# Two attention layers on one core: sums of two head groups at once, token maxima subtracted on VectorE, and another order of units in four slots

## The chip, the cores and the metric

The kernel runs on one core of one Trainium2 chip. The metric is the device time of one execution in microseconds (us). A core has TensorE (PE in the profile, its weight loads PEld), VectorE (DVE), ScalarE (ACT), GpSimd (POOL) and SyncE (SP), which run side by side, each through its own instructions in program order, and wait for each other on semaphores.

## The reference

Sixteen independent batches, each 112 query rows by 320 features, and a context of 375 rows by 192. Two layers of cross attention follow each other. Layer 0 has 8 heads of 40; of the 375 context rows the last 4 are tokens. Cut to what matters:

```python
# layer 0
hs      = mha(x @ Wq, enc @ Wk, enc @ Wv)            # enc: 371 rows, 8 heads
ca_q1   = einsum('btc,th->bch', ca, Wq_ca)[:, indices]
ca_hs1  = mha(ca_q1, x, x)                           # 112 x 112 scores, 8 heads
ca_hs2  = mha(ca_hs1 @ Wq, ca @ Wk_ca, ca @ Wv_ca)   # 4 tokens
x1      = (hs + ca_hs2) @ Wout + b_out + x
# layer 1: 20 heads of 16 over all 375 context rows
out     = mha(x1 @ Wq, ctx @ Wk, ctx @ Wv) @ Wo + bo + x1
```

## The kernel before, in words

The program is one software pipeline over the batches. An iteration `t` has seven slots. Each slot scores one **group** of four heads: slots 0 and 1 take the two groups of layer 0 of batch t (here a0, a1), slots 2 to 6 the five groups of layer 1 of batch t-1 (b0 to b4). A group passes through the engines in stages, one slot apart:

- `scores` (L1156, L1159): TensorE computes queries by keys, two heads (a pair) at a time, into the two PSUM banks `bankS`. VectorE takes the row maxima (`maximum`, L773) after each pair. The second pair may start only when the maxima of the first are taken.
- one slot later `transpose_m` (L1172) turns the negated maxima into a row, VectorE copies it out (`copy_mT`, L779) and a DMA places it as one more row of the queries.
- two slots later (`LAG` is 2) `shifted_scores` (L1187, L1193) computes keys by queries with the maximum already subtracted, ScalarE takes the exponentials (`exps`, L573, L574, L577), `attend` (L1225) multiplies them with the values into `bankO`, and VectorE copies the result out (`copy_o`, L790).

Between these stages stand the **units**: projections, transposes and small products (K1_0 is part 0 of the keys of layer 1, V0_1 part 1 of the values of layer 0, q0 the queries, q1T_0 a transpose of part of them, N0, N1a and N1b the transposes of the attention sums before they are divided by the sums of exponentials, out0 and out1 the output projections). All units share two PSUM banks, `bankX`, in turn: a unit gets the bank that the unit two before it in the written order had, and waits until ScalarE or VectorE, or one after the other, has emptied it. The order is written out by hand in the table `UNITS`: for each slot four phases of units, with the offset of the batch. On TensorE a slot runs

```python
scores(g, 0); units of phase 0; shifted_scores(late); transpose_m(before)
units of phase 1; scores(g, 1); units of phase 2; attend(late); units of phase 3
```

VectorE's slot is: maxima of pair 0, what phase 0 needs, `copy_mT`, phase 1, maxima of pair 1, phase 2, `copy_o`, phase 3. ScalarE's is: phase 0, `exps`, the DMA of the maxima, phases 1 to 3.

The drains that matter below: q1T is rounded by ScalarE (L666), then multiplied by VectorE (L829). q0 and q1 are rounded by ScalarE (L648, L653), the remainder is taken by VectorE (L765). K0 and K1 go through ScalarE (L625, L619) and VectorE (L814, L809), and DMAs then stack them for the scores of the next iteration (`stack_k0` on SP, L347; `stack_k1` on SP and GpSimd).

The 112 x 112 softmax of layer 0 are the units S2_0 and S2_1 (L1111), four heads each. VectorE takes the maxima (L837); then ScalarE runs one exponential per head with the maximum as bias and a sum beside it (L595), and this empties the bank. `reciprocal2` (L877) turns the sums over, GpSimd scales (`normalise2`, L464), and T2_0, T2_1 transpose. S3 and p3T are the four tokens' part; `normalise3` is its softmax's division (three small instructions, L881 to L885).

Of the kernel before, what the change touches and what calls it, by code (L numbers as in the profile page):

```python
# [7 lines left out]
ALU = mybir.AluOpType  # L8
# [51 lines left out]
    ([], [("T2_0", 0), ("T2_1", 0)], [("V0_0", 0), ("V0_1", 0), ("q0", 1)], [("V0_2", 0), ("PV2", 0), ("K1_0", 0)]),  # L60
# [25 lines left out]
NUMBER = {g: n for n, g in enumerate(GROUPS)}  # L86

# [24 lines left out]
def xattn_kernel(nc, xT, xpad, ctxT, caS, caT, w_all, w_ca, wqT, bd96, consts, bias, out):  # L112
    g_rows = nc.dram_tensor("g_rows", [B, 3, 32, HID], F32, kind="Internal").ap()

    with ExitStack() as ctx:
# [101 lines left out]
        bank_mT = bankO[0:GROUP, 0:SQ]  # L217
# [57 lines left out]
        rsum2_done = sem("rsum2_done")  # L275
        prob2_ready = sem("prob2_ready")
# [275 lines left out]
        def _(act):  # L552
# [10 lines left out]
            def exps(g):  # L563
# [4 lines left out]
                if n >= 2:  # L568
                    act.wait_ge(pv_done, n - 1)
                elif n == 1:  # L570
                    act.wait_ge(w_split, parts_split[2])
# [19 lines left out]
            def exps2(b, half):  # L591
                act.wait_ge(max2_done, 2 * b + half + 1)
                X = bankX[bank(f"S2_{half}", b)]
                for h in range(4 * half, 4 * half + 4):
                    last = nc.scalar.activation(prob2[0:SQ, h, :], X[0:SQ, (h % 4) * SQ:(h % 4 + 1) * SQ], ACT.Exp,  # L595
                                                bias=negmax2[:, h:h + 1], accum_out=sum2[:, h:h + 1])
                last.then_inc(bank_drained[bank(f"S2_{half}", b)], 1)

            def unit(name, b):
# [27 lines left out]
                elif kind == "V0":  # L627
                    if i == 0 and b == 0:
                        act.wait_ge(zeroed, 3)
                    elif i == 0:  # L630
                        act.wait_ge(pv_done, NUMBER[0, b - 1, 1] + 1)
# [3 lines left out]
                elif kind == "V1":  # L635
                    if i == 0 and b < 2:
                        act.wait_ge(zeroed, 6 + b)
                    elif i == 0:
                        act.wait_ge(pv_done, NUMBER[1, b - 2, G1 - 1] + 1)
# [91 lines left out]
        def _(dve):  # L731
# [49 lines left out]
            def copy_o(g):  # L781
                layer, b, k = g
                n = NUMBER[g]
                dve.wait_ge(pv_done, n + 1)
                if layer == 0:
                    dst, src = o0T[:, 2 * k:2 * k + 2, :].rearrange("p c q -> p (c q)"), bankO[:, 0:2 * SQ]
                else:
                    at = (2 + n % 2) * SQ
                    dst, src = o1T[:, k, :], bankO[:, at:at + SQ]
# [554 lines left out]
```

## Time and profile before

| what | value |
|---|---|
| median of three runs | 756.53 us (755.18 to 759.52) |
| the profiled execution | 753.38 us, span 751.5 us |
| TensorE busy | 703.0 us, 94% of the span |
| VectorE busy | 472.3 us, 63% |
| ScalarE busy | 404.0 us, 54% |
| GpSimd busy | 295.5 us, 39% |
| mean granted TensorE clock | 0.983 of full speed |

The span is what lies between the first and last instruction of the profile; the execution's own time is 1.9 us longer. TensorE's share is that of matmuls in flight, whose records overlap, so it is no measure of how fast it works, but what it leaves is time in which nothing was in flight.

### The profile page before, as it was taken

The page shows a single profiled execution, that of the slowest core. Times are in us where ns is not written, and L with a number is a line of the kernel's source. Part 1 is how long each engine was busy: PE and PEld are TensorE (multiplying, and loading weights), DVE is VectorE, ACT ScalarE, POOL GpSimd, SP SyncE. Part 2 cuts the span into 40 slices and gives each one's busy share as a digit, 9 for nine tenths or more (in the row PEclk, how much of TensorE's full clock was granted, in tenths as well). Part 3 has the DMA queues.
Part 4 walks back from the last instruction along what each step waited for, and adds up shares of the span by engine and source line. Part 5 has one row for each costly group of instructions (what it writes and reads, how often), then busy time and mean ns, then how long its engine had stood idle before and what let it go on. Part 6 is the DMA issues. An engine that isn't in the chain of part 4 may idle for free.

```text
span 751.5 us, 18194 instructions
## 1 busy us (share of the span) xinstructions
PE 703.0 (94%) x6924; PEld 610.3 (81%) x6924; DVE 472.3 (63%) x1028; ACT 404.0 (54%) x923; POOL 295.5 (39%) x401
## 2 busy tenths in 40 slices
PE   8787999999999999999999999999999999999975
PEld 5586888888888888888888888888888888888763
DVE  2653666657576665757576575756667575766662
ACT  2454555555565555565555555556555555654432
POOL 5485662444334253433325344323524542330300
PEclk9889999999999999999999999999999999999996
DMA  9533553443516244252524434261533425051400
GB/s 325 175 96 96 112 133 75 107 80 79 133 47 143 62 119 95 67 118 54 137 60 125 92 80 103 62 142 45 136 81 94 89 76 129 20 137 28 87 7 11
DMA packets 52387, 72.45 MB, mean 96 GB/s; under 512 B 12128, under 2 KB 44256, under 8 KB 52304
## 3 DMA queue, kind: packets, MB, share of 16 engines
q1 hardware_dynamic: 44832, 60.34, 31.7%
q0 software_dynamic: 6144, 9.25, 6.5%
q10 hardware_dynamic: 1328, 1.71, 0.6%
q8 instruction: 57, 0.93, 0.5%
q14 instruction: 26, 0.21, 0.1%
HBM read 20.60 MB, written 4.26 MB: 33 GB/s over the span
## 4 chain that ended last, share of the span: by engine, by line
PE 69%; ACT 13%; DVE 8%; issue 3%; POOL 1%; DMA 1%; SPq 1%; ACTq 0%; POOLq 0%
PE bankX L1005 28%; PE bankO L1225 8%; PE bankST L1193 7%; ACT arena L577 7%; PE bankS L1159 6%; PE bankST L1187 5%; ACT arena L595 3%; DVE negmax L773 2%; DVE q1T L829 2%; PE bankX L1118 2%; PE bankX L1125 2%; PE bankX L1087 2%; PE bankS L1156 2%; ACT q1T L666 2%; PE bankX L1071 2%
## 5 line engine op out<-in xcount | busy, mean ns | idle before, releaser
L773 DVE TENSOR_REDUCE negmax<-bankS 112x2 f32<-112x750 f32 (+1 forms) x224 | 208.7, 932 | 57.0 <-PE bankS L1159 32.7
L494 POOL DMA_DIRECT2D k_stack<-stage x192 | 96.6, 511 | 181.5 <-DVE stage L809 153.9
L577 ACT ACTIVATE arena<-bankST 125x1344 f32<-125x1344 f32 x80 | 103.5, 1294 | 30.9 <-PE bankST L1193 30.9
L1225 PE MATMUL bankO<-arena,v 125*32 125x112 f32 (+2 forms) x2688 | 107.2, 264 | 6.2 <-ACT arena L577 4.4
L1225 PEld LDWEIGHTS bankO<-arena,v 125*32 125x32 f32 (+2 forms) x2688 | 81.2, 117 | 29.0 <-issue 12.7
L1159 PE MATMUL bankS<-k_stack,q1T 112*112 112x376 f32 x320 | 87.8, 355 | 4.1 <-DVE negmax L773 3.0
L1005 PE MATMUL bankX<-ctx_hi,WH 128*120 128x376 f32 (+2 forms) x192 | 69.0, 360 | 3.0 <-DVE qn L765 2.2
L457 POOL TENSOR_TENSOR w2bd<-w2s,cst 96x896 fp32r<-96x896 f32 x16 | 29.9, 1870 | 98.4 <-DVE w2s L765 98.4
L1005 PE MATMUL bankX<-WH,ctx_hi 128*125 128x320 f32 x192 | 66.1, 344 | 0.1
L1193 PE MATMUL bankST<-q1T,k_stack 112*125 112x224 f32 x480 | 65.4, 272 | 0.0
L1005 PE MATMUL bankX<-ctx_hi,WL 128*120 128x376 f32 (+2 forms) x192 | 64.0, 334 | 0.0
L1193 PEld LDWEIGHTS bankST<-q1T,k_stack 112*125 112x125 f32 x480 | 62.0, 188 | 0.8 <-DMA q1T<-mT 0.4
L1005 PE MATMUL bankX<-WL,ctx_hi 128*125 128x320 f32 x192 | 58.5, 312 | 0.0
L1159 PEld LDWEIGHTS bankS<-k_stack,q1T 112*112 112x112 f32 x320 | 49.4, 177 | 8.8 <-DVE negmax L773 6.5
L829 DVE TENSOR_SCALAR q1T<-bankX,odd_rows 128x448 fp32r<-128x448 f32 (+1 forms) x48 | 29.1, 606 | 41.7 <-ACT q1T L666 41.2
L595 ACT ACTIVATE arena<-bankX,negmax 112x112 f32<-112x112 f32 x128 | 43.6, 354 | 21.7 <-DVE negmax L837 21.6
L1005 PE MATMUL bankX<-WH,act_hi 128*112 128x320 f32 x144 | 46.7, 325 | 3.3 <-DVE act_hi L866 1.4
L483 POOL TENSOR_TENSOR xb<-xp,bias_sb 112x320 f32<-112x320 f32 x16 | 13.9, 867 | 88.7 <-DVE x L860 88.6
L779 DVE CAST mT<-bankO 4x112 fp32r<-4x112 f32 x112 | 29.0, 259 | 30.0 <-PE bankO L1172 30.0
L1187 PEld LDWEIGHTS bankST<-q0T,k_stack 121*125 121x125 f32 (+1 forms) x384 | 46.0, 187 | 0.0
L619 ACT ACTIVATE stage<-bankX 128x376 fp32r<-128x376 f32 (+1 forms) x48 | 23.1, 482 | 41.7 <-PE bankX L1005 41.0
L1187 PE MATMUL bankST<-q0T,k_stack 121*125 121x112 f32 (+1 forms) x384 | 44.9, 266 | 0.0
(141 smaller groups left out, 1545.8 us busy)
## 6 DMA issues: line engine op xcount, KB each, us to landing
k_stack<-stage SPq DMA_DIRECT2D x96, 176.2 KB
k_stack<-stage SPq DMA_DIRECT2D x192, 70.5 KB, 2.6
k_stack<-stage POOLq DMA_DIRECT2D x192, 47.0 KB, 2.0
ctx_raw<-in_ctxT SPq DMA_DIRECT2D x16, 376.0 KB, 3.3
k_stack<-stage SPq DMA_DIRECT2D x48, 117.5 KB
xp<-in_xpad SPq DMA_DIRECT2D x16, 224.0 KB, 3.3
x_raw<-in_xT SPq DMA_DIRECT2D x16, 168.0 KB, 2.4
out<-x1b SPq DMA_DIRECT2D x16, 140.0 KB, 3.2
```

The costliest lines, as they stand in the source:

```text
L457: nc.gpsimd.tensor_tensor(w2bd[:, :, :], w2s[:, :].bitcast(F32).unsqueeze(1).broadcast_to((96, H0, SQ)), mask96.unsqueeze(2).broadcast_to( ...
L494: pool.dma_start(dst, src).then_inc(k1_stacked_pool[b % 2], 16)
L577: nc.scalar.activation(dst[0:KC], bankST[0:KC, :, 0:GROUP * SQ], ACT.Exp).then_inc(exp_done, 1)
L595: last = nc.scalar.activation(prob2[0:SQ, h, :], X[0:SQ, (h % 4) * SQ:(h % 4 + 1) * SQ], ACT.Exp, bias=negmax2[:, h:h + 1], accum_out=sum2 ...
L773: nc.vector.tensor_reduce(negmax[:, n % 2, 2 * pair:2 * pair + 2], bankS[0:SQ, :, 0:keys], axis=AX, op=ALU.max, negate=True).then_inc(max_ ...
L779: nc.vector.tensor_copy(mT[:, n % MT_BUFS, :], bank_mT).then_inc(mT_copied, 1)
L829: nc.vector.tensor_scalar(q1T[:, 4 * i:4 * i + g, 1, :], X[:, 0:g * SQ].rearrange("p (h q) -> p h q", h=g), odd_rows[:, :], None, ALU.mult ...
L1005: last = nc.tensor.matmul(dst, lhs, rhs, start=(n == 0), stop=(n == len(passes) - 1))
L1159: last = nc.tensor.matmul(bankS[0:SQ, j, 0:SKP], q1T[0:ROWS1, h // 2, h % 2, :], k1_stack[b % 2][0:ROWS1, h // 2, :], start=True, stop=True)
L1187: last = nc.tensor.matmul(bankST[0:keys, c, SQ * j:SQ * j + SQ], k0_stack[0:M_ROW0 + 1, h, KC * c:KC * c + keys], q0T[0:M_ROW0 + 1, h, :], ...
L1193: last = nc.tensor.matmul(bankST[0:KC, c, 2 * SQ * pair:2 * SQ * pair + 2 * SQ], k1_stack[b % 2][0:ROWS1, 2 * k + pair, KC * c:KC * c + KC ...
L1225: last = nc.tensor.matmul(dst, v, src[0:keys, c, SQ * j:SQ * j + SQ], start=(c == 0), stop=(c == NKC - 1))
```

## The change

It has five parts.

1. `attend` and `copy_o` work on an **episode**: the two groups of layer 0 together, of layer 1 groups 0 and 1, 2 and 3, and 4 alone. An episode is attended in the slot in which its last group's turn comes: slot 3 (a0, a1), slot 5 (b0, b1), slot 0 (b2, b3), slot 1 (b4). Semaphores count episodes.
2. The transposed maxima move from `bankO` to spare columns of the second bank of `bankS`. `transpose_m` therefore waits for the maxima of pair 0 of the group that is being scored now, and the second matmul of each `scores` waits for `copy_mT`. `attend` and `transpose_m` no longer wait for each other's copies.
3. In S2 VectorE subtracts the maxima while it copies the scores out of the bank (an added tensor_tensor of 112 x 448 for each half), which frees the bank; ScalarE then runs one exponential of 448 columns in place for each half.
4. `reciprocal2` sums the exponentials on VectorE first (an added reduction of 112 x 896) and stands at the end of slot 3; it stood in slot 4, behind `copy_mT`.
5. The table of units is another one in slots 1 to 4, and the first slots likewise.

```diff
 UNITS = [
     ([("V1_0", -1)], [("q1T_0", -1)], [("V1_1", -1)], [("W2", 1), ("PV2", 0)]),
-    ([("q1T_1", -1), ("V1_2", -1)], [("q1T_2", -1)], [("q0", 1)], [("N1a", -2), ("K1_0", 0)]),
-    ([("K1_1", 0)], [("S3", 0), ("S2_0", 1)], [("N1b", -2)], [("S2_1", 1)]),
-    ([("K1_2", 0)], [("K0_0", 1)], [("hn1T", -2)], [("K0_1", 1)]),
-    ([("K0_2", 1)], [("p3T", 0), ("N0", 0)], [("out1", -2)], [("q0T_0", 1)]),
+    ([("q1T_1", -1), ("V1_2", -1)], [("q1T_2", -1), ("N1a", -2)], [("q0", 1)], [("S2_0", 1)]),
+    ([("K1_0", 0)], [("S3", 0)], [("N1b", -2), ("S2_1", 1)], [("K1_1", 0)]),
+    ([("K1_2", 0)], [("K0_0", 1)], [("hn1T", -2)], []),
+    ([("K0_1", 1)], [("out1", -2)], [("p3T", 0), ("N0", 0)], [("K0_2", 1), ("q0T_0", 1)]),
     ([("hn0T", 0), ("V0_0", 1)], [("q0T_1", 1)], [("out0", 0)], [("T2_0", 1)]),
     ([("x1T", 0), ("V0_1", 1)], [("T2_1", 1)], [("q1", 0)], [("V0_2", 1)]),
 ]
 FIRST_SLOTS = [
     ([], [], [], [("W2", 1)]),
-    ([], [("T2_0", 0), ("T2_1", 0)], [("V0_0", 0), ("V0_1", 0), ("q0", 1)], [("V0_2", 0), ("PV2", 0), ("K1_0", 0)]),
+    ([], [("T2_0", 0), ("T2_1", 0)], [("V0_0", 0), ("V0_1", 0), ("q0", 1)], [("V0_2", 0), ("PV2", 0)]),
+    ([("K1_0", 0)], [("S3", 0)], [("S2_0", 1)], [("K1_1", 0), ("S2_1", 1)]),
 ]
...
+EPISODES = [e for b in range(B + 1) for e in
+            ([[(0, b, 0), (0, b, 1)]] if b < B else []) +
+            ([[(1, b - 1, 0), (1, b - 1, 1)], [(1, b - 1, 2), (1, b - 1, 3)], [(1, b - 1, 4)]] if b > 0 else [])]
+EPISODE = {g: n for n, e in enumerate(EPISODES) for g in e}
...
-        bank_mT = bankO[0:GROUP, 0:SQ]
+        bank_mT = bankS[0:GROUP, 1, SKP + 8:SKP + 8 + SQ]
...
             def exps2(b, half):
-                act.wait_ge(max2_done, 2 * b + half + 1)
-                X = bankX[bank(f"S2_{half}", b)]
-                for h in range(4 * half, 4 * half + 4):
-                    last = nc.scalar.activation(prob2[0:SQ, h, :], X[0:SQ, (h % 4) * SQ:(h % 4 + 1) * SQ], ACT.Exp,
-                                                bias=negmax2[:, h:h + 1], accum_out=sum2[:, h:h + 1])
-                last.then_inc(bank_drained[bank(f"S2_{half}", b)], 1)
+                act.wait_ge(bank_drained[bank(f"S2_{half}", b)], drained(f"S2_{half}", b))
+                scores2 = prob2[0:SQ, 4 * half:4 * half + 4, :].rearrange("p h k -> p (h k)")
+                nc.scalar.activation(scores2, scores2, ACT.Exp).then_inc(exp2_done, 1)
...
+                    nc.vector.tensor_tensor(
+                        prob2[0:SQ, 4 * i:4 * i + 4, :], X[0:SQ, 0:4 * SQ].rearrange("p (h k) -> p h k", h=4),
+                        negmax2[:, 4 * i:4 * i + 4].unsqueeze(2).broadcast_to((SQ, 4, SQ)), ALU.add).then_inc(free, 1)
...
             def reciprocal2(b):
-                dve.wait_ge(bank_drained[bank("S2_0", b)], drained("S2_0", b))
-                dve.wait_ge(bank_drained[bank("S2_1", b)], drained("S2_1", b))
+                dve.wait_ge(exp2_done, 2 * b + 2)
+                nc.vector.reduce_sum(sum2[:, :], prob2[0:SQ], axis=AX).then_inc(sum2_done, 1)
+                dve.wait_ge(sum2_done, b + 1)
                 nc.vector.reciprocal(rsum2[:, :], sum2[:, :]).then_inc(rsum2_done, 1)
...
-                    if i == 4 and t + 1 < B:
-                        reciprocal2(t + 1)
...
-                    if late:
-                        copy_o(late)
+                    if attended_at(t, i):
+                        copy_o(attended_at(t, i))
                     for u in units_of(t, i, 3):
                         unit(*u)
                     if i == 2 and t < B:
                         normalise3(t)
                     if i == 3 and t < B:
                         split_p3(t)
+                    if i == 3 and t + 1 < B:
+                        reciprocal2(t + 1)
...
                 for j in range(2):
                     h = GROUP * k + 2 * pair + j
+                    if j == 1 and transposed > 0:
+                        pe.wait_ge(mT_copied, transposed)
...
-            def transpose_m(g, attended):
+            def transpose_m(g, scoring):
                 n = NUMBER[g]
-                pe.wait_ge(max_done, 2 * n + 2)
+                if scoring:
+                    pe.wait_ge(max_done, 2 * NUMBER[scoring] + 1)
+                else:
+                    pe.wait_ge(max_done, 2 * n + 2)
                 if n > 0:
                     pe.wait_ge(mT_copied, n)
-                else:
-                    pe.wait_ge(g_split, 4)
-                if attended > 0:
-                    pe.wait_ge(o_copied, attended)
```

The matmuls of `attend` are the same and as many, in the same order within a group.

## Rows read from the trace of the kernel before

**Rows 1.** The page's head: span, and busy time, share and instructions by engine.
```profile
span 751.5 us, 18194 instructions
PE 703.0 (94%) x6924; PEld 610.3 (81%) x6924; DVE 472.3 (63%) x1028; ACT 404.0 (54%) x923; POOL 295.5 (39%) x401
```

**Rows 2.** Timeline of PE over iteration 7: start, duration, instruction, idle before it.
```profile
329.13 0.51 PE L1156 MATMUL bankS<-k_stack,q0T 120*112 120x372 f32 x2
...
333.54 0.82 PE L1105 MATMUL bankX<-x_raw,bd 128*96 128x112 f32 x6 [0.25 <-DVE q1T L829]
...
338.13 0.31 PE L1005 MATMUL bankX<-WH,x_hi 128*112 128x320 f32 x1
...
340.93 0.45 PE L1005 MATMUL bankX<-ctx_hi,WH 128*128 128x376 f32 x1 [0.17 <-DVE qn L765]
...
347.86 0.46 PE L1111 MATMUL bankX<-w2bd,ca_st 96*112 96x448 f32 x1 [0.33 <-ACT arena L595]
...
357.27 0.65 PE L1095 MATMUL bankX<-cst,o0T 128*112 128x128 f32 x4 [0.49 <-DVE stage L814]
...
370.93 0.78 PE L1225 MATMUL bankO<-arena,v 125*32 125x112 f32 x24
...
372.48 0.50 PE L1156 MATMUL bankS<-k_stack,q0T 120*112 120x372 f32 x2
```

**Rows 3.** The chain that ended last, in order of time, same iteration.
```profile
346.35 1.46 ACT arena L595 x8
...
348.31 0.35 PE bankS L1159 x2
348.66 0.85 PE bankX L1005 x5
349.51 1.24 PE bankST L1187 x12
...
352.35 1.31 PE bankO L1225 x24
...
362.67 0.65 PE bankST L1193 x6
```

**Rows 4.** Timeline of ACT, slot 1 of the iteration.
```profile
337.62 1.29 ACT L577 ACTIVATE arena<-bankST 125x1344 f32<-125x1344 f32 x1 [0.21 <-PE bankST L1193]
...
338.81 0.34 ACT L666 ACTIVATE q1T<-bankX 64x224 fp32r<-64x224 f32 x1
```

**Rows 5.** Timeline of DVE, same iteration.
```profile
339.18 0.45 DVE L829 TENSOR_SCALAR q1T<-bankX,odd_rows 128x224 fp32r<-128x224 f32 x1 [1.21 <-ACT q1T L666]
...
347.29 0.22 DVE L797 TENSOR_TENSOR hn<-bankX,r 112x64 f32<-112x64 f32 x1
...
371.77 0.49 DVE L765 SCALAR_TENSOR_TENSOR qn<-bankX,qn 112x320 fp32r<-112x320 f32 x1 [0.97 <-ACT qn L653]
```

**Rows 6.** Groups of instructions: busy us, mean ns of one, then idle before.
```profile
L773 DVE TENSOR_REDUCE negmax<-bankS 112x2 f32<-112x750 f32 (+1 forms) x224 | 208.7, 932 | 57.0 <-PE bankS L1159 32.7 <-PE bankS L1156 24.2
...
L790 DVE COPY o1T<-bankO 128x112 f32<-128x112 f32 x80 | 21.5, 269 | 12.9 <-PE bankO L1225 12.9
...
L837 DVE TENSOR_REDUCE negmax<-bankX 112x4 f32<-112x448 f32 x32 | 19.8, 620 | 5.8 <-PE bankX L1111 5.7
...
L574 ACT ACTIVATE arena<-bankST 121x448 f32<-121x448 f32 x32 | 17.2, 538 | 0.0
...
L790 DVE COPY o0T<-bankO 128x224 f32<-128x224 f32 x32 | 12.5, 392 | 3.2 <-PE bankO L1225 2.0
...
L860 DVE TENSOR_TENSOR x<-bankX,xb 112x320 f32<-112x320 f32 x16 | 7.9, 492 | 7.9 <-PE bankX L1005 7.9
...
L885 DVE TENSOR_TENSOR p<-p,rsum 112x32 f32<-112x32 f32 x16 | 3.1, 191 | 0.6
```

**Rows 7.** Timeline of SP, same iteration.
```profile
357.29 8.46 SPq L347 DMA_DIRECT2D k_stack<-stage  x9
```

**Rows 8.** DMA issues by line: count, KB each, median us to landing.
```profile
k_stack<-stage SPq DMA_DIRECT2D x192, 70.5 KB, 2.6
```

More of the change, by code:

```diff
@@ L275, in xattn_kernel @@
         rsum2_done = sem("rsum2_done")
+        exp2_done = sem("exp2_done")
+        sum2_done = sem("sum2_done")
         prob2_ready = sem("prob2_ready")
@@ L911, in _ @@
                 for i in range(SLOTS):
-                    g, before, late = scored_at(t, i), scored_at(t, i, 1), scored_at(t, i, LAG)
+                    g, before = scored_at(t, i), scored_at(t, i, 1)
                     if g:
@@ L1090, in unit @@
                     layer, k = {"N0": (0, 1), "N1a": (1, 3), "N1b": (1, 4)}[kind]
-                    pe.wait_ge(o_copied, NUMBER[layer, b, k] + 1)
+                    pe.wait_ge(o_copied, EPISODE[layer, b, k] + 1)
                     cols = [o0T[:, c, :] for c in range(4)] if layer == 0 else [
@@ L1135, in unit, with scores @@
                 last.then_inc(unit_filled, 1)
-            def scores(g, pair):
+            def scores(g, pair, transposed):
                 layer, b, k = g
@@ L1225, in attend @@
-                    last = nc.tensor.matmul(dst, v, src[0:keys, c, SQ * j:SQ * j + SQ], start=(c == 0),
-                                            stop=(c == NKC - 1))
+                        at_once = [(c, j) for pair in range(2) for c in range(NKC) for j in (2 * pair, 2 * pair + 1)]
+                    else:
+                        at_once = [(c, j) for c in range(NKC) for j in range(GROUP)]
+                    for c, j in at_once:
+                        h = GROUP * k + j
+                        if layer == 0:
+                            keys = KC if c < 2 else KC - NTOK
+                            at = (2 * k + j // 2) * SQ
+                            dst = bankO[64 * (j % 2):64 * (j % 2) + 64, at:at + SQ]
+                            v = v0[0:keys, c, 64 * h:64 * h + 64]
+                        else:
+                            keys = KC
+                            at = (2 + k % 2) * SQ
+                            dst = bankO[32 * j:32 * j + 32, at:at + SQ]
+                            v = v1[b % 2][0:keys, c, 32 * h:32 * h + 32]
+                        last = nc.tensor.matmul(dst, v, src[0:keys, c, SQ * j:SQ * j + SQ], start=(c == 0),
+                                                stop=(c == NKC - 1))
@@ L1249, in _ @@
                     if g:
-                        scores(g, 0)
+                        scores(g, 0, transposed)
                     for u in units_of(t, i, 0):
@@ L1255, in _ @@
                     if before:
-                        transpose_m(before, attended)
+                        transpose_m(before, g)
                         transposed = NUMBER[before] + 1
@@ L1260, in _ @@
                     if g:
-                        scores(g, 1)
+                        scores(g, 1, transposed)
                     for u in units_of(t, i, 2):
                         unit(*u)
-                    if late:
-                        attend(late, transposed)
-                        attended = NUMBER[late] + 1
+                    if attended_at(t, i):
+                        attend(attended_at(t, i))
                     for u in units_of(t, i, 3):
```

58 lines of the change are left out of this document (26 added, 32 removed).

## The prediction

> **What bounds the kernel now.** I read the page's head first, then TensorE's timeline over one whole iteration, then what filled each gap there on the other engines. The head says that something is in flight on TensorE for 94% of the span, VectorE is busy for 63% and ScalarE for 54% [rows 1]. So TensorE's order of work sets the time, and another engine matters only where TensorE stands and waits for it. One iteration takes 372.48 - 329.13 = 43.35 us [rows 2], and the iterations 1 to 14, the full ones, repeat it.
>
> The timeline shows four places in it where TensorE is empty [rows 2]: W2 waits 0.25 us for VectorE's drain of q1T_0; K1_0 waits 0.17 for VectorE's drain of q0; S2_1 waits 0.33 for ScalarE's eight instructions of S2_0, which take 1.46 us in all [rows 3]; N0 waits 0.49 for VectorE's drain of K0_2. All four are the same thing: a unit waits for its turn of `bankX`, because the unit two before it has not been emptied. They add up to 1.24 us. Matmuls overlap by some 0.15 us at each of these places, and some waits are too short to empty the engine, so I estimate what such waits cost at 2.4 us of the 43.35, with 1.24 as the lower bound.
>
> **The change part by part.** TensorE's matmuls stay as they are. What can change is only the waiting, so I walk through an iteration in the new order, with a unit's two-before neighbour looked up each time.
>
> *What is removed.* In the new order W2 has 24 more matmuls of an episode ahead of it (the second group adds about 0.7 us, from the duration 0.78 in [rows 2]), and its 0.25 goes. S2_0's bank is free after two VectorE instructions, the 0.620 maxima [rows 6] and the subtraction. I take 0.62 for that too: 320 columns take 0.492 and the step from 112 to 224 columns of a copy costs 0.123, 1.1 ns a column [rows 6], so 448 give 0.63. That replaces 1.46 on ScalarE, and S2_1 no longer stands directly behind. N0 now has out1 two before it instead of K0_2. All of the 2.4 us goes. Three of seven changeovers into `attend` go as well: no row prices one, it lies between nothing and a matmul's own latency of about 0.26, and I take 0.1 each and 0.35 in all with those behind it. Removed: 2.75 us, bounds 1.2 and 3.2.
>
> On ScalarE eight instructions per half become one of 0.54 [rows 6], worth about 1 us each half. It was idle beside TensorE there, so this is worth nothing by itself. On VectorE copies shrink (a copy of 448 columns is about 0.64 instead of two of 0.392 [rows 6]), some 0.4 us less an iteration; the two subtractions add 1.25, the reduction over 896 columns about 1.09 (0.932 for 750 [rows 6] and 146 more at 1.1 ns; 1.11 if all of it scales). VectorE is idle for some 16 us of an iteration (37%, [rows 1]), so the question is only where these stand.
>
> *New wait 1, q0 behind q1T_2.* The order was q1T_1, V1_2, q1T_2, q0, so q0 had V1_2 two before it. It becomes q1T_1, V1_2, q1T_2, N1a, q0: q0 has q1T_2 before it. That one's drain is late, because ScalarE reaches it only behind `exps` of b4: those start at 337.62, q1T_2's at 338.81 [rows 4], VectorE's part starts 339.18 and ends 339.63 [rows 5]. Nothing ahead of this moves. q0 started at 338.13 [rows 2]; with N1a's four transposes (0.65, of which 0.26 overlaps what follows) in front it could start at 338.5, and must now wait until 339.7. Cost 1.15 us. This is the surest of all terms: both times are read.
>
> *New wait 2, K1_1 behind N1b.* In slot 2 the order is K1_0, S3, N1b, S2_1, K1_1, and no `attend` stands in that slot any more. N1b is emptied by VectorE only behind the maxima of b0's second pair: 0.932, then a reciprocal of about 0.2 and a product of 0.22 [rows 5, 6], with handoffs 1.45 us after the scores end. TensorE has N1b and S2_1 to do meanwhile, under 0.5 us. Cost 0.95, bounds 0.6 and 1.1.
>
> *New wait 3, transposing the maxima in slot 3.* `transpose_m` now waits for the maxima of the group just scored. In slot 3 these are queued on VectorE behind: maxima and subtraction of S2_1 (1.25), the wait for ScalarE, which is in order itself and does the exponential of S2_1 (0.54) before it rounds K1_1 (0.5 for 376 columns against 0.54 for 448), VectorE's part of K1_1 (0.55: 0.492 and 56 columns more), `normalise3` (three at 0.19), and their own 0.932 [rows 6]. Together 4.2 us from the end of N1b's drain, with some overlap. TensorE, released by that same drain, has K1_1, scores, K1_2 and the shifted scores: 0.9 + 0.35 + 0.85 + 1.24 [rows 3], 3.4 us with a changeover. Cost 0.8, bounds 0.4 and 1.1. Behind the waiting transpose stands everything on TensorE.
>
> *New wait 4, the same in slot 4.* The double `attend` of layer 0 (twice 1.31 [rows 3]) ends slot 3. Behind it VectorE must copy 448 columns (0.64), split p3 (0.19), sum 896 columns (1.09), take the reciprocal (0.2), and only then take the maxima of b2's first pair (0.932): 3.0 us. TensorE has scores, K0_1 and the shifted scores of b0: 0.35 + 0.9 + 0.65 [rows 3], 2.0 us. Cost 1.05, bounds 0.6 and 1.2. The Trainium skill ("VectorE: DVE Perf Modes", Rules for kernel authors) advises to expect 1x of `tensor_reduce` on a hot path and calls it the slowest VectorE operation; its cycle table (The AWS errata-adjusted cycle table, same page) would give 0.99 us as an estimate for this one, so by the page this wait would be 0.95. No row here has the reduction itself.
>
> *Smaller ones.* V1_0 waits for q1, whose drain the `attend` of slot 6 [rows 2] used to cover: VectorE ends it at 371.77 + 0.49 [rows 5], TensorE would be there 0.36 earlier. N0 now follows out1 and scores so closely that its bank is 0.3 late. K0_2 moves from before N0 to the end of slot 4, and hn0T, two behind it, has only q0T_0 and scores as cover: 0.4. q0T_0 behind N0 0.15; slot 2's S2_1 behind S3 and K1_0 0.25. Together 1.45, bounds 0.7 and 2.0. The second matmul of each `scores` waits for `copy_mT`, which comes 0.6 us after the transpose, just when a unit of transposes and one matmul have passed; I take nothing, and 0.1 in each of three slots as the bound.
>
> *Sum.* Added 1.15 + 0.95 + 0.8 + 1.05 + 1.45 = 5.4, removed 2.75: 2.65 us an iteration. Fourteen full iterations: 37 us. At the two ends I estimate 2 more: in the last slots, with no units, `copy_mT` (about 0.26, the size of the 0.269 copy [rows 6]) now stands between the maxima of the two pairs, for five groups, and the first reciprocal waits for a reduction. The profiled execution took 753.38 us, so 792.5; the median of the runs shown is 3 us above it. I predict 795.
>
> **The rivals.**
>
> *Faster: the new waits are covered.* The place is VectorE's queue in slots 2 to 4: if it ran ahead of TensorE there, waits 2 to 4 would vanish, and if ScalarE took q1T_2 ahead of `exps`, wait 1 too. Then only the removals count: 2.75 x 14 = 38, 718 us. The point from which it decides is added waits under 2.75 an iteration. For it speaks that VectorE is idle 37% of the time [rows 1]; against it that each queue is strictly in order and wait 1 alone, read from recorded times, takes 1.15 of it. Somewhere between (waits at their lower bounds, removals at their upper) lies 756 to 762. The Trainium skill ("Perfetto Trace Analysis", Identifying the Most-Contended Engine) ranks engines by occupancy and has the busiest optimised first; by that alone, work moved to an engine at 63% would cost nothing and this rival would hold.
>
> *Slower by less: waits 3 and 4 fall away.* If the second one's reduction and the drains of S2 run shorter than the rows suggest, or if TensorE arrives later for another reason, 1.85 an iteration goes: 795 - 26 = 769.
>
> *Slower by more: stacking K0 comes late.* K0_2's drain moves some 6 us later. The nine DMAs of `stack_k0` take 8.46 us to issue on SP [rows 7], behind that drain, and the last lands 2.6 us after its issue [rows 8]. By the walk they land less than 1 us before the next a0 is scored. If it takes 2 us more, each iteration is 1 us longer: 809.
>
> *It does nothing:* the two sides cancel, 753 to 760.
>
> **How the numbers follow.** Forecast with its own range 778 to 806: 0.66. K0 late: 0.10. Waits 3 and 4 gone: 0.10. Nothing: 0.05. Faster: 0.09. A change under 0.5%, 3.8 us, can't be told from none by a measurement of this kernel. The range takes in the first three cases: 764 to 812. Faster 0.09, same 0.05, slower 0.86.
>
> **What the profile after would show.** An iteration of about 46 us. TensorE empty before q0 for some 1.1 us with VectorE's L829 as the one waited for; before K1_1, for the drain of N1b; before the transpose of the maxima in slots 3 and 4, for the maxima, 0.8 and 1.0; none of the four gaps of now. VectorE busy some 30 us longer, ScalarE some 50 shorter. The prediction is wrong if the transposes find the maxima done, or if the iteration is 43 or less.

## The result, and the profile after

| | before | changed |
|---|---|---|
| median of five runs | 755.85 us (754.58 to 759.52) | 807.72 us (806.28 to 813.15) |
| profiled execution, span | 753.38, 751.5 us | 813.15, 811.3 us |
| mean granted TensorE clock | 0.983 | 0.952 |

The ratio is 1.0688, interval 1.0644 to 1.0732: slower by 52 us, where the forecast was 39. The median lies outside the forecast's own range of 778 to 806 and inside the outer one, which reached to 812. The profiled execution of the changed kernel was its slowest run, 5.4 us above the median.

The head of the page of the changed kernel, to set beside [rows 1]:

```profile
span 811.3 us, 17904 instructions
PE 726.3 (90%) x6924; PEld 629.5 (78%) x6924; DVE 502.6 (62%) x1028; ACT 375.5 (46%) x699; POOL 294.6 (36%) x401
```

VectorE is busy 30 us longer, ScalarE 28.5 shorter. The forecast said 50, but its own working (about 1 us less for each of 32 halves) gives 32. TensorE has as many matmuls and is in flight 23 us longer; the reason for that comes below.

TensorE's timeline over one iteration, to set beside [rows 2]:

```profile
312.79 0.82 PE L1124 MATMUL bankX<-x_raw,bd 128*96 128x112 f32 x6
...
317.39 0.59 PE L1177 MATMUL bankS<-k_stack,q0T 120*112 120x372 f32 x2
318.93 0.40 PE L1024 MATMUL bankX<-WH,x_hi 128*112 128x320 f32 x1 [0.95 <-DVE q1T L841]
...
325.44 0.46 PE L1130 MATMUL bankX<-w2bd,ca_st 96*112 96x448 f32 x1
326.73 0.44 PE L1024 MATMUL bankX<-ctx_hi,WH 128*128 128x376 f32 x1 [0.83 <-DVE hn L809]
...
330.88 0.26 PE L1192 MATMUL bankS<-cst,negmax 112*4 112x112 f32 x1 [0.59 <-DVE negmax L786]
...
332.63 2.54 PE L1248 MATMUL bankO<-arena,v 125*64 125x112 f32 x48
...
338.03 0.26 PE L1192 MATMUL bankS<-cst,negmax 112*4 112x112 f32 x1 [0.82 <-DVE negmax L786]
...
340.11 0.65 PE L1114 MATMUL bankX<-cst,o0T 128*112 128x128 f32 x4
...
342.75 0.51 PE L1106 MATMUL bankX<-cst,hn 112*128 112x112 f32 x3 [0.22 <-DVE stage L826]
...
354.11 0.57 PE L1177 MATMUL bankS<-k_stack,q0T 120*112 120x372 f32 x2 [0.31 <-issue]
```

The four gaps of before are gone: W2 (312.79) follows its attend without one, K1_0, S2_1 (325.44) and N0 (340.11) too. In their place stand four others, each at the named place: q0 waits 0.95 us for VectorE's part of q1T_2; K1_1 waits 0.83 for N1b's drain; the transposes of the maxima in slots 3 and 4 wait 0.59 and 0.82. Counted from where the instruction could have started they cost a little more, as a matmul's latency overlaps the rest: q0 could have gone at 317.80 (the scores start at 317.39 and take 0.41), and goes 1.13 later.

VectorE's timeline shows what is queued in front of the last two:

```profile
326.45 0.22 DVE L809 TENSOR_TENSOR hn<-bankX,r 112x64 f32<-112x64 f32 x1
...
327.24 0.62 DVE L855 TENSOR_TENSOR arena<-bankX,negmax 112x448 f32<-112x448 f32 x1
328.87 0.55 DVE L821 TENSOR_TENSOR stage<-bankX,stage 128x376 fp32r<-128x376 f32 x1 [1.01 <-ACT stage L632]
...
329.90 0.93 DVE L786 TENSOR_REDUCE negmax<-bankS 112x2 f32<-112x750 f32 x1
...
335.21 0.62 DVE L802 COPY o0T<-bankO 128x448 f32<-128x448 f32 x1 [0.55 <-PE bankO L1248]
335.75 0.18 DVE L910 TENSOR_TENSOR p3w<-p,p3w 112x32 fp32r<-112x32 f32 x1
335.85 1.08 DVE L894 TENSOR_REDUCE sum<-arena 112x8 f32<-112x896 f32 x1
336.97 0.20 DVE L896 RECIPROCAL rsum<-sum 112x8 f32<-112x8 f32 x1
337.09 0.89 DVE L786 TENSOR_REDUCE negmax<-bankS 112x2 f32<-112x750 f32 x1
```

Before 329.90 it sits idle for 1.01 us itself, for ScalarE's rounding of K1_1, and the maxima stand behind that. Before 337.09 stand the copy, the split, the sum and the reciprocal. The three operations that no row of before had came out as estimated: 0.62 (0.62), 0.62 (0.64) and 1.08 (1.09). For the sum the cycle table of the Trainium skill ("VectorE: DVE Perf Modes", The AWS errata-adjusted cycle table) gives an estimate of 0.99 us; the trace has 1.08, so here the table is 0.09 short.

I take an iteration from the first matmul of W2 in it to that in the next. Between iterations 1 and 14 there are thirteen such stretches. The first, in which the pipeline isn't yet full, takes 43.1 us (before 40.6). Of the twelve full iterations behind it four take 46.1 us and eight 46.6 to 47.2; before it was 43.3 in all twelve. The difference between the two kinds is in the clock. The windows by stretch (length, busy time of the five engines, granted clock, DMA), first two whole iterations, then two short stretches inside the second:

```profile
312.79:358.88 46.09, 42.23 (x431) 37.05 (x427) 30.30 (x64) 22.91 (x43) 17.11 (x24) 1.00 0.37 89
358.88:405.49 46.61, 43.35 (x432) 38.33 (x428) 30.41 (x64) 22.85 (x43) 17.09 (x24) 0.96 0.36 86
...
372.00:374.00 2.00, 1.18 (x4) 1.19 (x5) 1.88 (x5) 0.02 (x1) 0.00 (x0) 0.59 0.00 1
374.00:376.00 2.00, 2.00 (x9) 1.98 (x8) 0.66 (x3) 1.04 (x2) 0.00 (x0) 0.56 0.04 8
```

The clock fell while TensorE still waited for K1_1's bank (the wait ends at 372.82): in windows of half a microsecond it is 0.86 of full speed from 372.0, then 0.50, the lower of the two levels (1.2 GHz), until 375.5. Matmuls of 376 columns follow each other every 0.31 us instead of 0.17. Part of that time comes back: the transpose in slot 3, which then arrives late, no longer waits 0.59 for its maxima. This is also why TensorE's busy time grew with the same matmuls: a full iteration at the full clock is busy 42.2 us here and 42.0 before, the one from 358.88 on 43.35, and the rest of the growth is at the two ends, which come below.

### The profile page after: what moved, and what is told of

Read it like the earlier page. It is cut to its first block, busy times and chain, and to the rows that moved or that the text cites. A ratio compares the mean times of both kernels' runs of the same rounds, so it can differ in the third digit from the quotient of the medians.

```text
span 811.3 us, 17904 instructions
## 1 busy us (share of the span) xinstructions
PE 726.3 (90%) x6924; PEld 629.5 (78%) x6924; DVE 502.6 (62%) x1028; ACT 375.5 (46%) x699; POOL 294.6 (36%) x401
## 4 chain that ended last, share of the span: by engine, by line
PE 69%; DVE 15%; ACT 5%; issue 3%; POOL 1%; DMA 1%; SPq 1%; ACTq 0%; POOLq 0%
PE bankX L1024 27%; PE bankO L1248 11%; PE bankST L1213 5%; PE bankS L1180 5%; DVE negmax L786 5%; PE bankST L1207 4%; PE bankS L1177 3%; ACT arena L593 2%; PE bankX L1106 2%; DVE sum L894 2%; PE bankX L1137 2%; PE bankX L1144 2%; PE bankS L1192 2%; PE bankX L1152 1%; PE bankX L1097 1%
## 5 line engine op out<-in xcount | busy, mean ns | idle before, releaser
L1180 PE MATMUL bankS<-k_stack,q1T 112*112 112x376 f32 x320 | 96.4, 380 | 6.5 <-DVE negmax L786 4.1
L1248 PE MATMUL bankO<-arena,v 125*32 125x112 f32 (+2 forms) x2688 | 99.1, 265 | 2.7 <-ACT arena L593 2.7
L1024 PE MATMUL bankX<-ctx_hi,WH 128*120 128x376 f32 (+2 forms) x192 | 75.1, 391 | 12.8 <-DVE hn L809 10.8
L1024 PE MATMUL bankX<-ctx_hi,WL 128*120 128x376 f32 (+2 forms) x192 | 68.8, 358 | 0.0
L1180 PEld LDWEIGHTS bankS<-k_stack,q1T 112*112 112x112 f32 x320 | 53.4, 186 | 15.0 <-DVE negmax L786 6.6
L638 ACT ACTIVATE stage<-bankX 120x376 fp32r<-120x376 f32 (+1 forms) x48 | 23.2, 484 | 78.2 <-PE bankX L1024 78.2
L1024 PEld LDWEIGHTS bankX<-ctx_hi,WH 128*120 128x120 f32 (+2 forms) x192 | 37.8, 197 | 22.1 <-DVE hn L809 14.5
L1207 PEld LDWEIGHTS bankST<-q0T,k_stack 121*125 121x125 f32 (+1 forms) x384 | 48.8, 197 | 0.0
L1177 PE MATMUL bankS<-k_stack,q0T 120*112 120x372 f32 x128 | 39.0, 387 | 10.3 <-issue 8.4
L826 DVE TENSOR_TENSOR stage<-bankX,stage 120x376 fp32r<-120x376 f32 (+1 forms) x48 | 26.1, 544 | 34.4 <-ACT stage L638 34.4
```

Source lines behind the costliest of these rows:

```text
L826: nc.vector.tensor_tensor(k0_lo[0:rows, i, :].bitcast(F32R), X[0:rows, 0:SKP], k0_hi[0:rows, i, :], ALU.subtract).then_inc(free, 1)
L1024: last = nc.tensor.matmul(dst, lhs, rhs, start=(n == 0), stop=(n == len(passes) - 1))
L1177: last = nc.tensor.matmul(bankS[0:SQ, j, 0:SKE + 1], q0T[0:M_ROW0, h, :], k0_stack[0:M_ROW0, h, 0:SKE + 1], start=True, stop=True)
L1180: last = nc.tensor.matmul(bankS[0:SQ, j, 0:SKP], q1T[0:ROWS1, h // 2, h % 2, :], k1_stack[b % 2][0:ROWS1, h // 2, :], start=True, stop=True)
L1207: last = nc.tensor.matmul(bankST[0:keys, c, SQ * j:SQ * j + SQ], k0_stack[0:M_ROW0 + 1, h, KC * c:KC * c + keys], q0T[0:M_ROW0 + 1, h, :], ...
L1248: last = nc.tensor.matmul(dst, v, src[0:keys, c, SQ * j:SQ * j + SQ], start=(c == 0), stop=(c == NKC - 1))
```

## The experiments

Each kernel is compared with the kernel before on the same chip. The first W2 starts 17 to 18 us into the span in nine of the fourteen profiled executions and at 22 us in five, whatever the edit, and this moves a median by several microseconds. So beside the median I give the time of a full iteration, from W2 to W2, as the twelve of the profiled execution have it.

### One part at a time

**The new table of units alone.** The two tables as in the diff above, all else as before:

```diff
-    ([("q1T_1", -1), ("V1_2", -1)], [("q1T_2", -1)], [("q0", 1)], [("N1a", -2), ("K1_0", 0)]),
+    ([("q1T_1", -1), ("V1_2", -1)], [("q1T_2", -1), ("N1a", -2)], [("q0", 1)], [("S2_0", 1)]),
...
```

> The kernel before with the new table of units and first slots alone. Theory A (each wait comes from one part meeting another): of the new waits only q0 behind q1T_2 (1.1 us) and hn0T behind K0_2 (0.3) and late stacked K0 appear; K1_1's wait for N1b stays covered, since attend of a0 still stands in slot 2, and the transposes of the maxima wait for nothing. Against that go some 1.2 us of old waits. Net 0 to +1 us an iteration: 756 to 772, best 764. Rival B (the order alone carries the loss): 795 or more.

Measured: 781.64 us, ratio 1.0343 (1.0293 to 1.0394), an iteration 44.8. So the order alone costs 1.5 us an iteration; theory A named the right places, but 781.64 lies 10 us above its range: its 0 to 1 us an iteration was 0.5 to 1.5 too hopeful. Rival B (795 or more) falls. TensorE's timeline has q0 and hn0T where they were expected:

```profile
350.29 0.40 PE L1006 MATMUL bankX<-WH,x_hi 128*112 128x320 f32 x1 [0.95 <-DVE q1T L830]
...
365.64 0.60 PE L1160 MATMUL bankS<-k_stack,q1T 112*112 112x376 f32 x2 [0.36 <-DVE negmax L774]
...
373.13 0.51 PE L1088 MATMUL bankX<-cst,hn 112*128 112x112 f32 x3 [0.42 <-DVE stage L815]
```

q0's wait is 0.95 us here as in the changed kernel. It needs nothing but the new neighbour in the table.

**All but the table.** The changed kernel with the two tables of before:

```diff
-    ([("q1T_1", -1), ("V1_2", -1)], [("q1T_2", -1), ("N1a", -2)], [("q0", 1)], [("S2_0", 1)]),
+    ([("q1T_1", -1), ("V1_2", -1)], [("q1T_2", -1)], [("q0", 1)], [("N1a", -2), ("K1_0", 0)]),
...
```

> The changed kernel with the tables of before. Theory A: the wait of q0 and that of K1_1 for N1b go, the waits of the transposes for the maxima stay, the one in slot 4 longer (1.5 us, since VectorE's part of K0_1 now lies in front of the sum of 896 columns), and S2_1 has lost its cover in slot 2: 770 to 790. Rival B (order alone carries the loss): 750 to 758.

Measured: four runs of 846.8, 875.9, 877.2 and 879.1 us, with mean granted clocks of 0.90 in the first and 0.86 in the others. Both theories missed by far. What follows is read from the fastest of them. The waits came as theory A had them, the transpose of slot 4 and S2_1:

```profile
341.35 0.46 PE L1129 MATMUL bankX<-w2bd,ca_st 96*112 96x448 f32 x1 [0.87 <-DVE arena L854]
...
357.91 0.26 PE L1191 MATMUL bankS<-cst,negmax 112*4 112x112 f32 x1 [1.43 <-DVE negmax L785]
```

What nobody had priced is the clock. The windows of two whole iterations of the 846.8 us execution:

```profile
327.85:379.04 51.19, 48.19 (x431) 42.90 (x427) 30.36 (x64) 23.17 (x43) 17.16 (x24) 0.87 0.34 80
...
428.91:474.64 45.73, 42.38 (x431) 37.20 (x427) 30.24 (x64) 23.01 (x43) 17.16 (x24) 1.00 0.38 91
```

With the full clock the iteration takes 45.7, 2.4 more than before (two of the twelve); with the clock at half in parts of it, 48.2 to 51.2 (the other ten, mean clock 0.87 to 0.93). The waits cost 2.4, the slower clock up to 5.5. So the parts don't add up. The table costs 1.5 us an iteration on the kernel before, but only 0.4 on top of the other parts (46.1 against 45.7 at the full clock); and with it the granted clock in a full iteration of the change is 0.96 or 1.00. Without the table the change is slower still. Its two longest waits are 0.87 and 1.43 us, against 0.95 and 0.83 with it, but that this is why the clock differs is not shown.

**The subtraction on VectorE and the early sum alone.** Before, with parts 3 and 4 of the change:

```diff
-                    if i == 4 and t + 1 < B:
-                        reciprocal2(t + 1)
...
+                    if i == 3 and t + 1 < B:
+                        reciprocal2(t + 1)
```

> The kernel before with the subtraction on VectorE, one exponential for each half, and the sum of 896 columns at the end of slot 3, nothing else. Theory A: S2_1's 0.33 goes, N0 waits some 1 us longer for K0_2's drain, which VectorE reaches behind the sum: 0 to +1 us an iteration, 756 to 770, best 764. Rival C (VectorE and ScalarE work beside a TensorE-bound kernel is free, and only the four gaps count): 750 to 754.

Measured: 774.54 us, ratio 1.0245 (1.0202 to 1.0288), an iteration 44.5, 1.1 more than before, and the median is 5 us above theory A's range. S2_1's gap is gone and N0's is 1.54 in place of 0.49 [rows 2]:

```profile
327.29 0.65 PE L1101 MATMUL bankX<-cst,o0T 128*112 128x128 f32 x4 [1.54 <-DVE stage L813]
```

The 1.05 us more at N0 is the size expected; the 0.33 did not come back as a gain. Rival C falls: VectorE had 37% to spare and its extra work still cost 1.1 us an iteration.

**Episodes and the moved maxima alone.** The changed kernel with the old tables, the old S2 and the old `reciprocal2` (its edits are the `attend`, `copy_o`, `scores` and `transpose_m` of the diff above):

```diff
-        bank_mT = bankO[0:GROUP, 0:SQ]
+        bank_mT = bankS[0:GROUP, 1, SKP + 8:SKP + 8 + SQ]
...
```

> The kernel before with episodes and the transposed maxima in the scores' bank (with their waits), old table, old S2. Theory A: W2's wait and three changeovers go (0.7 us an iteration), S2_1 loses the attend that covered the exponentials of S2_0 (+1.3), V1_0 loses its cover (+0.4), one transpose waits 0.4: +1.4 an iteration, 770 to 785, best 776. Rival D (fewer and longer attends are a gain as such): 745 to 752.

Measured: 788.4 us in one run and 801.7 to 806.5 in three, mean clocks 0.956 and 0.934 to 0.938. Even the fastest run is above the range expected. The trace is of a run of 803.8 us. In it an iteration with the full clock takes 44.25, 0.9 more than before (expected 1.4); that is seven of the twelve, the other five take 45.7 to 48.4. Rival D falls. S2_1 now waits for the eight exponentials without an attend in front:

```profile
324.08 0.71 PE L1123 MATMUL bankX<-w2bd,ca_st 96*112 96x448 f32 x1 [1.69 <-ACT arena L608]
```

and in this iteration the clock falls during the wait and stays at half for some 10 us, while TensorE is full:

```profile
322.00:324.00 2.00, 0.39 (x3) 0.13 (x1) 1.70 (x5) 1.70 (x10) 0.00 (x0) 0.74 0.00 1
324.00:326.00 2.00, 1.92 (x6) 1.84 (x7) 1.10 (x5) 0.54 (x4) 0.00 (x0) 0.50 0.00 0
326.00:328.00 2.00, 2.00 (x11) 2.00 (x9) 1.33 (x3) 1.42 (x7) 0.00 (x0) 0.50 0.00 0
```

The same wait of 1.69 us stands in all twelve full iterations; in seven of them the clock stays at 1.00.

**The moved maxima alone.** Before, with the transposed maxima in the scores' bank and the waits that belong to it, one group at a time:

```diff
+                    if j == 1 and transposed > 0:
+                        pe.wait_ge(mT_copied, transposed)
...
-                pe.wait_ge(max_done, 2 * n + 2)
+                if scoring:
+                    pe.wait_ge(max_done, 2 * NUMBER[scoring] + 1)
+                else:
+                    pe.wait_ge(max_done, 2 * n + 2)
```

> The kernel before with the transposed maxima in the scores' bank and nothing else: the transpose waits for the first maxima of the group being scored, the second matmul of each scores for the copy. Theory A: in a full iteration the maxima are done in time except in slot 4 (0.3 us, inside the gap before N0 that is there anyway), so iterations stay within 0.5 us of 43.35; in the last two iterations, where no units lie between, each of some nine slots is 0.3 to 0.6 longer: 758 to 764. Rival G (these waits cost something at each of the seven slots): 1 us an iteration or more, 770 or more.

Measured: 761.57 us, ratio 1.0069 (1.0037 to 1.0101), an iteration 43.4. Theory A holds, rival G falls. From the last W2 to the end of the span it takes 120.3 us, before 114.7: of the 7.6 us by which the two profiled executions differ (759.1 and 751.5 us), 5.6 are in the last iterations. What they consist of is read below, with the two ends.

### Undoing one wait at a time

**N1a ahead of q1T_2:**

```diff
-    ([("q1T_1", -1), ("V1_2", -1)], [("q1T_2", -1), ("N1a", -2)], [("q0", 1)], [("S2_0", 1)]),
+    ([("q1T_1", -1), ("V1_2", -1)], [("N1a", -2), ("q1T_2", -1)], [("q0", 1)], [("S2_0", 1)]),
```

> The changed kernel with N1a ahead of q1T_2 in slot 1, so that q0 has N1a two before it. Theory A (q0's wait is that of the bank that q1T_2 holds, and its time is lost): q0's 1.1 us becomes 0.4 at most, 13 times, some 9 us off: 798. Rival E (the queues behind catch up, so a wait removed here comes back as a longer one in slots 2 to 4): 804 to 808.

**The sum back behind the copy of the maxima in slot 4:**

```diff
-                    if i == 3 and t + 1 < B:
-                        reciprocal2(t + 1)
...
                         copy_mT(before)
+                    if i == 4 and t + 1 < B:
+                        reciprocal2(t + 1)
```

> The changed kernel with the sum of 896 columns and the reciprocal back in slot 4 behind the copy of the transposed maxima. Theory A (the transpose in slot 4 waits for the maxima because the sum stands ahead of them): its 0.82 us goes, N0 and q0T_0 lose 0.1 to 0.2 of it, and 10 us go: 797. Rival E: 804 to 808.

**K1_1 ahead of S2_1:**

```diff
-    ([("K1_0", 0)], [("S3", 0)], [("N1b", -2), ("S2_1", 1)], [("K1_1", 0)]),
+    ([("K1_0", 0)], [("S3", 0)], [("N1b", -2), ("K1_1", 0)], [("S2_1", 1)]),
```

> The changed kernel with K1_1 ahead of S2_1 in slot 2. Theory A: K1_1's 0.83 us of waiting for N1b's drain falls to under 0.3 for S2_1, K1_2 waits up to 0.4, and with the long wait goes the half clock that follows it in 10 of the 14 iterations (all iterations near 46 us): 790 to 797. Rival F (the half clock comes from the load of the stretch and not from this wait): iterations of 46.8 and 47.2 us stay, 799 to 803. Rival E: 804 to 808.

**All three:**

> The changed kernel with all three edits: N1a ahead of q1T_2, K1_1 ahead of S2_1, the sum behind the copy of the maxima. Theory A (the new waits are in series and each costs its own time): the three gains add up, 770 to 778. Rival E: one of them sets the pace and the sum of the gains is not reached: 785 or more.

| edit | median | an iteration, full clock / with the lower | expected |
|---|---|---|---|
| none (the change) | 807.72 | 46.1 / 46.6 to 47.2 (eight of twelve) | |
| N1a first | 800.09 | 45.4 / 46.0 to 46.5 (five) | 798 |
| sum after the maxima | 806.32 | 45.5 / 46.1 to 46.2 (four) | 797 |
| K1_1 first | 799.53 | 45.6 / none | 790 to 797 |
| all three | 779.90 | 44.2 / none | 770 to 778 |

Taken by the iteration at full clock, the edits save 0.7, 0.6 and 0.5 us, and all three 1.9: the waits are in series, each costs its own time, and rival E falls. The medians show the first and the third: no run of either is as slow as the fastest of the change (806.28). The second's 806.3 (runs of 799.5 to 809.0) lies where rival E put it and doesn't show its 0.6. Its profiled execution has the first W2 at 22.3 us, 4.9 later than the change's; from the first W2 to the end of the span it takes 784.7 us, the change 793.9. That is one trace of each, and I don't take a gain in the total from it as shown. All four medians are above what was expected, by 2 to 9 us. With K1_1 first the windows show the full clock in all twelve iterations, where the changed kernel has it in four, so that rival F falls too:

```profile
216.09:261.60 45.51, 42.51 (x432) 37.00 (x428) 30.30 (x64) 23.06 (x43) 17.12 (x24) 1.00 0.38 89
261.60:307.45 45.85, 42.50 (x431) 37.03 (x428) 30.31 (x64) 22.95 (x43) 17.12 (x24) 1.00 0.37 88
307.45:353.04 45.59, 42.53 (x431) 37.06 (x427) 30.30 (x64) 22.95 (x43) 17.13 (x24) 1.00 0.38 89
```

The wait in slot 4 is still 0.82 us long there, and q0's 0.95. In the changed kernel all eight falls come at the wait before K1_1, of 0.83. But that wait alone doesn't decide it: it is still 0.83 long in all twelve iterations of the kernel with N1a first, which has five falls, and of the one with the sum after the maxima, which has four. Why it falls there, and in these iterations, the runs don't tell.

**The parts of K0 back in their places, on top of the three:**

```diff
-    ([("K1_2", 0)], [("K0_0", 1)], [("hn1T", -2)], []),
-    ([("K0_1", 1)], [("out1", -2)], [("p3T", 0), ("N0", 0)], [("K0_2", 1), ("q0T_0", 1)]),
+    ([("K1_2", 0)], [("K0_0", 1)], [("hn1T", -2)], [("K0_1", 1)]),
+    ([("K0_2", 1)], [("out1", -2)], [("p3T", 0), ("N0", 0)], [("q0T_0", 1)]),
```

> The kernel with three edits, and K0_1 and K0_2 also back where they stood before (end of slot 3, start of slot 4). Theory A (K0_2's drain at the end of slot 4 brings the stacked K0 late): the waits in front of a0's first scores (2.3 us before iteration 1, 0.3 to 0.8 in others) and of hn0T (0.2) go, 0.5 us an iteration and 3 at the start: 768 to 773. Rival H (those waits are not the stacked K0's): they stay, 777 to 781.

Measured: 774.92 us, ratio 1.0257 (1.0200 to 1.0315), an iteration 44.1. The median is 2 us above what was expected. The wait in front of the first scores of iteration 1, with the three edits and here:

```profile
78.74 0.57 PE L1177 MATMUL bankS<-k_stack,q0T 120*112 120x372 f32 x2 [2.39 <-issue]
```

```profile
78.67 0.56 PE L1177 MATMUL bankS<-k_stack,q0T 120*112 120x372 f32 x2 [0.24 <-issue]
```

The profile names no one for it, but moving K0_1 and K0_2, and nothing else, takes 2.15 of the 2.39 us away, and with it the wait of hn0T and the 0.3 us before slot 0. With the new table alone the wait is there too (2.25 us); in the changed kernel it is 2.30, in the kernel before 0.67. Rival H falls. In a full iteration the gain is only 0.1, less than the 0.5 expected: V1_0's wait for q1, which the late K0 had covered, comes out (a gap of 0.21 us), and the transpose in slot 4 waits 0.25 again.

### What the change offers, on the kernel before

**The subtraction on VectorE, with the sum late in slot 4:**

```diff
+                    if i == 4 and t + 1 < B:
+                        reciprocal2(t + 1)
                     if (t, i) == (0, 0):
                         reciprocal2(0)
```

(The line stands at the end of the slot, behind phase 3; the rest as in the variant with the early sum.)

> The kernel before with the subtraction on VectorE and one exponential for each half, the sum of 896 columns at the end of slot 4, behind the copy of the attention sums. Theory A (what the sum costs depends on what stands behind it on VectorE): the 1.05 us that N0 waited longer in the variant with the sum in slot 3 goes, S2_1's gap stays closed: iterations of 42.9 to 43.3, 748 to 754. Rival I (VectorE's extra 1.9 us an iteration cost as such): 760 or more.

Measured: 761.14 us, ratio 1.0058 (1.0028 to 1.0088), an iteration 43.6. Theory A missed; the number is where rival I put it. Step by step against the timeline of before, S2_1 starts 0.42 us earlier, and this is gone again by slot 4. Then the sum pushes VectorE's split of hn0T, and q0T_1, which has that bank, starts 0.25 later:

```profile
367.92 1.08 DVE L881 TENSOR_REDUCE sum<-arena 112x8 f32<-112x896 f32 x1
369.03 0.20 DVE L883 RECIPROCAL rsum<-sum 112x8 f32<-112x8 f32 x1
369.15 0.89 DVE L772 TENSOR_REDUCE negmax<-bankS 112x2 f32<-112x750 f32 x1
369.95 0.38 DVE L868 TENSOR_TENSOR act_lo<-bankX,act_hi 128x224 fp32r<-128x224 f32 x1
```

**The same, with out1 ahead of p3T and N0:**

```diff
-    ([("K0_2", 1)], [("p3T", 0), ("N0", 0)], [("out1", -2)], [("q0T_0", 1)]),
+    ([("K0_2", 1)], [("out1", -2)], [("p3T", 0), ("N0", 0)], [("q0T_0", 1)]),
```

> The same, and out1 ahead of p3T and N0 in slot 4, so that N0 has out1 two before it instead of K0_2. Theory A: N0's 0.49 us gap shrinks to 0.3 or less and out1's wait for p3T's drain goes: 0.6 us an iteration, 740 to 746. Rival I as above; rival J (out1 in front only moves the wait to N0 and hn0T): within 2 us of the other.

Measured: 752.06 us over twelve runs, against 754.97 of before on the same chip; ratio 0.9954 (0.9924 to 0.9985), an iteration 43.0 in place of 43.3. It is the only version that beats the kernel before, by 0.5%, and the median is 6 us above the range expected. N0's gap is gone. Against the variant without the swap it saves 0.57 us an iteration, as expected (0.6), so rival J falls; what was wrong was the base it starts from. Rival I falls here as well: VectorE's extra work is the same, and the time isn't 760 or more.

## Why the prediction was right, and where it was short

The forecast of 795 was 13 us short, and the measured median is above the range of 778 to 806 that went with it. It lies inside the outer range only because that took in the rival of the late K0 at 809, which came in part; the larger share of what was missing is TensorE's clock. That the outer range held is luck. What the working got right is the full iteration.

**What bounds the kernel.** Right: in a full iteration of the changed kernel every recorded gap but one is the drain of a `bankX` unit or the maxima, and each was found by looking up the unit two before. The one is that before the first scores, the late K0.

**What is removed.** Right in place; all four gaps went. The 2.75 us can't be read singly, and neither can the 5.4 of what was added: only their difference is measured, so errors of the same size in both would not show. The expectations for the single parts, worked out in the same way, were 0.5 to 1.5 us an iteration too low for the table, 0.3 to 0.7 too low for the late sum and 0.5 too high for the episodes. That the whole came within 0.2 is better than the method shows itself to be elsewhere here.

**New waits 1 to 4.** Predicted 1.15, 0.95, 0.8 and 1.05 us. Measured from the start that would have been possible: 1.13 for q0; 1.0 for K1_1, with a recorded gap of 0.83; recorded gaps of 0.59 and 0.82 for the two transposes, some 0.2 more each with the latency that overlaps. Undoing q0's, K1_1's and slot 4's took 0.7, 0.5 and 0.6 us off the iteration; each left smaller waits behind (0.23 to 0.28 before q0, 0.2 before K1_2, and 0.57 before N0 where 0.1 to 0.2 was expected). That each wait costs time of its own is therefore shown by its own experiment, except for slot 3's, which was undone only together with K1_1's; the full sizes put for them are read from the timeline.

**Smaller ones.** hn0T waits 0.22 where 0.4 was put, N0 too little to leave a gap. V1_0's was hidden behind the late K0 and came out when that was mended.

**Iteration.** Predicted 46.0 (43.35 + 2.65), measured 46.1 with the full clock. The thirteen intervals from W2 to W2 of iterations 1 to 14 took 602.7 us, before 560.4: 42.4 more, where 34 follow from 2.65. Some 6 of the 8 us between are the clock, which no term had: in eight iterations it fell to half at K1_1's wait.

**K0 late.** A rival with a chance of 0.10, and it happened in part: 0.3 to 0.8 us before the first scores of the iterations and 2.30 before iteration 1, where the kernel before has 0.67. Moving K0 back gave 0.1 us in a full iteration, where the rival put 1, and 5 us in the median, where it put 14. The walk had it land with less than 1 us to spare.

**The two ends: this is the term that was mis-sized.** "At the two ends I estimate 2 more". Up to the W2 of iteration 1 the changed kernel lost 6.2 us, and from the last W2 to the end 11.2, of which some 3 belong to the rest of iteration 14, which was counted as full. That leaves 14 us against 2. More than half of the two growths is not waiting at all: the matmuls are the same, and TensorE is busy with them 3.5 of the 6.2 us longer at the start and 6.3 of the 11.2 at the end, at a lower granted clock. From the last W2 on, before and changed:

```profile
636.79:751.50 114.71, 98.45 (x1036) 82.87 (x1036) 69.84 (x155) 50.65 (x99) 21.47 (x32) 0.95 0.22 48
```

```profile
685.35:811.30 125.95, 104.73 (x1040) 88.16 (x1036) 71.57 (x150) 49.02 (x85) 21.38 (x32) 0.88 0.22 46
```

At the start the wait for the stacked K0 is 1.6 us longer than before. Taken alone, three of the parts lengthen the first iteration, from W2 to W2: 43.7 us before, 45.4 with the new table, 44.9 with the early sum, 47.5 with episodes (at a clock of 0.80, before 0.87); with the maxima moved it is 43.3. At the end the kernel that only moves the maxima takes 5.6 us more. The mechanism named for it was `copy_mT` between two maxima, at the copy's own 0.26 us in five slots. The waits are there, and longer; in the changed kernel's last iterations the second matmul waits for the whole round, maxima, transpose and copy:

```profile
757.20 0.43 PE L1180 MATMUL bankS<-k_stack,q1T 112*112 112x376 f32 x1 [0.66 <-DVE mT L792]
...
762.67 0.43 PE L1180 MATMUL bankS<-k_stack,q1T 112*112 112x376 f32 x1 [0.44 <-DVE mT L792]
```

But they are not where most of the 5.6 us went. The last stretch of both kernels, from the same scores to the end, before and with the maxima moved:

```profile
715.62:751.50 35.88, 23.69 (x248) 17.86 (x248) 16.88 (x38) 9.93 (x13) 0.00 (x0) 0.84 0.03 9
```

```profile
719.02:759.10 40.08, 27.99 (x248) 20.99 (x248) 17.34 (x38) 9.96 (x13) 0.00 (x0) 0.72 0.03 8
```

What TensorE does not fill is 12.2 us in the one and 12.1 in the other; the same 248 matmuls take 4.3 us longer, and the clock is 0.72 in place of 0.84. So 1.4 of the 5.6 us are lost before this stretch, at the full clock, and 4.2 in it, to the clock. That is read from one trace of each kernel. Why the clock is lower there, and what remains of the growth of both ends, wasn't tried singly.

**The other rivals.** "Faster" fell: the four waits are in the timeline, and their recorded gaps alone add up to 3.2 us an iteration, above the 2.75 from which it turns. That work moved to an engine at 63% costs nothing doesn't hold here: the variant with only the S2 edits adds 32 us of VectorE work and takes 20 us more. "Waits 3 and 4 fall away" fell too: both are in the timeline.

## What to carry to other kernels

Where units take turns in two banks and every engine runs in order, an edit of the order is priced by walking it: for each unit, who had its bank, and what stands ahead of that one's drain in each queue. The share of busy time of the draining engine says nothing about it. Such a walk of one full iteration came within 0.2 us for the whole change, and missed by up to 1.5 for single parts. The pipeline's fill and drain need a walk of their own, since there the cover is missing that the full iteration gives. And new waits can cost in TensorE's clock as well, here from nothing to some 4 us for a single wait, so read the granted clock beside the time. A long operation in a queue, such as the sum of 896 columns, goes where nothing behind it is due for its length; if there is no such place, it isn't free.

## What the runs showed of the hardware that was not expected

A single wait of TensorE was followed by the lower of its two clock levels, but not dependably. In the kernel before, whose longest gap in a full iteration is 0.52 us, the granted clock is 1.00 in all twelve. In the changed kernel it fell at the gap of 0.83 us before K1_1 in eight of twelve iterations, to 0.50 for some 3 us; at S2_1's 1.69 us in the episodes-only kernel in five of twelve, in one of them for some 10 us with TensorE busy for nearly all of it, and that iteration took 48.4 us in place of 44.25. It isn't a matter of the gap's length alone: the same gaps stand in the iterations at full clock, N0's 1.54 us in the kernel with only the S2 edits was followed by a fall in one of twelve, and 0.95 us before q0 in none.

It also fell with no gap in front. These are the windows of the kernel with N1a first, in the stretches before its first W2, beside the same of the changed kernel (17.4 us to its first W2).

```profile
8.00:13.00 5.00, 5.00 (x23) 3.37 (x21) 1.45 (x4) 1.00 (x1) 3.40 (x3) 0.93 1.03 403
13.00:18.00 5.00, 5.00 (x18) 3.91 (x19) 1.60 (x4) 0.00 (x0) 3.00 (x5) 0.50 1.04 346
```

```profile
8.00:13.00 5.00, 5.00 (x29) 3.71 (x28) 2.34 (x6) 1.00 (x1) 3.30 (x3) 1.00 1.04 407
13.00:18.00 5.00, 4.69 (x30) 3.90 (x29) 1.67 (x5) 1.34 (x3) 3.18 (x6) 1.00 1.03 373
```

Up to 13 us TensorE is as busy in the one as in the other; in the first the clock goes to half from 12 us on, and the first W2 comes 4.6 us later. The runs of the kernel before also form two groups, 753.3 to 755.6 and 759.0 to 760.8 us on one chip. That this is the same thing is likely, but no kernel was profiled in both.
